# Attention in a four-stage network: two-part fp32r queries and keys, half of the projections among the score units, and DMAs moved between queues

## The reference

```python
attn = softmax(einsum('bhqd,bhkd->bhqk', q * SCALE, k), axis=-1)
out = einsum('bhqk,bhkd->bhqd', attn, v)        # then a projection
```

## Time and profile before

| | |
|---|---|
| median of the runs | 9524.35 us |
| profiled execution | 9521.44 us, span of its core 9519.6 us |
| mean granted TensorE clock | 0.838 of full speed |
| busy: PE, DVE, ACT, POOL | 7285.6, 5233.4, 3309.5, 1466.3 us |
| DMA | 298.52 MB in 158940 packets, mean 31 GB/s |

### The profile page before, as it was taken

One profiled execution on the slowest core, in us unless ns is written; L12 is line 12 of the kernel. 1 busy time (PEld: TensorE's weight loads), 2 busy tenths in 40 slices (PEclk: granted clock), 3 DMA queues, 4 the chain that ended last, 5 costly groups with the idle time before them and its releaser, 6 DMA issues.

```text
span 9519.6 us, 103202 instructions
## 1 busy us (share of the span) xinstructions
PE 7285.6 (77%) x32648; PEld 2877.3 (30%) x32648; DVE 5233.4 (55%) x5444; ACT 3309.5 (35%) x3706; POOL 1466.3 (15%) x700
## 2 busy tenths in 40 slices
PE   6779777797777977679776797777977779777797
PEld 1233322333223332233322333223332233322332
DVE  6575355743566536664366643666536664366643
ACT  3424334243332433324333243332433324333243
POOL 0230002300023010230102301032000320003200
PEclk8879877888887988888888888888988888888888
DMA  2001110011100111001110011100111001110011
GB/s 61 8 27 32 44 43 7 27 32 44 43 7 27 32 44 45 6 27 32 44 45 6 27 32 46 43 5 27 33 46 43 5 27 32 46 43 5 27 33 49
DMA packets 158940, 298.52 MB, mean 31 GB/s; under 512 B 48974, under 2 KB 56390, under 8 KB 158378
## 3 DMA queue, kind: packets, MB, share of 16 engines
q1 hardware_dynamic: 158378, 291.44, 10.2%
HBM read 185.75 MB, written 83.50 MB: 28 GB/s over the span
## 4 chain that ended last, share of the span: by engine, by line
PE 48%; DVE 20%; issue 14%; DMA 5%; DVEq 4%; ACT 4%; SPq 3%; POOL 1%; ACTq 0%; POOLq 0%
PE px L607 10%; PE ring L557 6%; PE ring L584 6%; DVE mx L764 4%; PE ring L560 4%; DVE hs L1262 4%; PE ring L586 3%; PE px L1022 3%; PE ring L1007 3%; DMA ks<-k_split 2%; PE ring L536 2%; PE ring L982 2%; DVE hs L1251 2%; PE ring L996 2%; DVEq L779 2%
## 5 line engine op out<-in xcount | busy, mean ns | idle before, releaser
L764 DVE TENSOR_REDUCE mx<-ring 128x1 f32<-128x1024 f32 (+1 forms) x1920 | 2158.0, 1141 | 2023.8 <-PE ring L560 968.0
L677 ACT ACTIVATE pt<-ring 128x1024 f32<-128x1024 f32 (+1 forms) x1920 | 1874.4, 982 | 2592.8 <-PE ring L586 1109.1
L824 POOL TENSOR_TENSOR os<-oe 64x512 f32<-64x512 f32 x288 | 365.2, 1268 | 6542.8 <-ACT oe L685 6542.8
L607 PE MATMUL px<-pt,vo 128*32 128x512 f32 (+3 forms) x8064 | 1258.4, 616 | 72.8 <-ACT pt L677 72.1
L557 PE MATMUL ring<-kb,qb 96*128 96x512 bf16 x3072 | 1184.3, 430 | 151.0 <-DVE mx L764 80.7
L1307 POOL TENSOR_TENSOR hc<-hs,crep 128x1024 f32<-128x1024 f32 x384 | 1045.4, 2722 | 1460.3 <-DVE hs L1262 1422.0
L584 PE MATMUL ring<-qb,kb 99*128 99x512 bf16 x3072 | 1116.4, 407 | 182.3 <-DVE mx L764 111.9
L560 PE MATMUL ring<-hot,rq 128*128 128x512 f32 x1536 | 901.7, 648 | 0.0
L1262 DVE TENSOR_TENSOR_SCAN hs<-ring,hs 128x1024 f32<-128x1024 f32 x384 | 874.9, 2278 | 1.5 <-ACT ring L1155 1.5
L586 PE MATMUL ring<-rq,hot 128*128 128x512 f32 x1536 | 861.7, 623 | 0.0
L1007 PE MATMUL ring<-duh,spread 96*128 96x512 f32 x1536 | 633.5, 525 | 278.0 <-DVE hs L1251 158.8
(11 more groups left out here) (154 smaller groups left out, 6756.0 us busy)
## 6 DMA issues: line engine op xcount, KB each, us to landing
qs<-q_split SPq DMA_DIRECT2D x192, 128.0 KB
q_parts<-part SPq DMA_DIRECT2D x96, 192.0 KB, 3.5
k_parts<-part SPq DMA_DIRECT2D x96, 192.0 KB, 2.7
qb<-q_parts SPq DMA_DIRECT2D x192, 96.0 KB
kb<-k_parts SPq DMA_DIRECT2D x192, 96.0 KB
ocm<-os SPq DMA_DIRECT2D x576, 32.0 KB
rb<-reciprocals SPq DMA_DIRECT2D x288, 64.0 KB, 2.2
qb<-q_parts SPq DMA_DIRECT2D x192, 64.0 KB
```

The source lines that it names most:

```text
L607: last = nc.tensor.matmul(m.px[32 * g:32 * g + 32, h % 2, lo - f * HF:hi - f * HF], m.vo[:, t, h, :], pt[:, lo - q0:hi - q0], start=t == t ...
L677: nc.scalar.activation(pt, ps, ACT.Exp, scale=1.0 if L == "C" else HD ** -0.5).then_inc(s.pt, 1)
L764: nc.vector.tensor_reduce(out, ps, AX.X, ALU.max).then_inc(s.mx_used, 1)
```

## The change

1. q and k are split in two fp32r parts in A and C as well, as in D. Scores there multiply 48 rows (`qs`, `ks`), weights 50 rows (48 and two of maxima) in place of 96 and 99 bf16 rows. The relative matmuls and D's masks are as before. Maxima have two parts everywhere. The ones under the keys come by DMA at the start of A and C.
2. Only jobs 0 and 1 are done before the first score. `LATE` puts the token projections (two units of four tiles) and jobs 2 and 3 with A's rotations in ring slots among the score units 2 to 11. All four head loads are issued together, before jobs 2 and 3 are split.
3. In C and D ACT writes `hi` straight from PSUM and DVE `lo` from PSUM; in A ACT writes `hi` from the rotated tile. The copies of v to `vo` move from DVE to ACT. The v bias is folded into the projection's bias at the start of the program.
4. The cosine product of the rotation moves from DVE to POOL.
5. In A and C `values` stands before each odd-numbered weights unit (from 3 on), not after each even-numbered one.
6. Of `px` ACT copies one half (`odd`), and DVE adds the other from PSUM to `os`. POOL issues the result's DMAs to `ocm`, SP the denominators' alone, on a semaphore of their own.
7. In C the position rows for D are loaded into each buffer after its last head, at h = 8 to 11, not at h = 2 to 5.

```diff
-STORED = {"A": (16 * 6, 16 * 6), "C": (16 * 10, 16 * 6), "D": (16 * 4, 16 * 4)}
+STORED = 16 * 4
...
+LATE = {2: ("tokens", 0), 4: ("tokens", 1), 6: ("job", 2), 8: ("rotated", 2), 9: ("job", 3), 11: ("rotated", 3)}
...
-                last = nc.tensor.matmul(out[:, half], m.qb[u][0:BR, q], m.kb[u][0:BR, half],
+                last = nc.tensor.matmul(out[:, half], m.qs[u][0:QR, q], m.ks[u][0:QR, half],
                                         start=True, stop=L == "A")
...
-                last = nc.tensor.matmul(out[:, half], m.kb[u][:, k], m.qb[u][:, half], start=True, stop=L == "A")
+                last = nc.tensor.matmul(out[:, half], m.ks[u][0:QR + MR, k], m.qs[u][0:QR + MR, half],
+                                        start=True, stop=L == "A")
...
+    for i in range(2):
+        job(i)
+    if L == "A":
+        for i in range(2):
+            rotated(i)
...
     for n in range(total + lead):
+        for kind, i in late(L, n):
+            if kind == "tokens":
+                tokens(i)
+            if kind == "job":
+                job(i)
+            if kind == "rotated":
+                rotated(i)
         for h, axis in relatives(L, n):
             relative(h, axis)
...
+            if L != "D" and g % 2 == 1 and g >= 3:
+                values(*divmod(g // 2 - 1, steps // 2))
             weights(g)
             if L == "D" and g >= 1:
                 values(*divmod(g - 1, steps))
-            if L != "D" and g % 2 == 0 and g >= 2:
-                values(*divmod(g // 2 - 1, steps // 2))
...
-        nc.scalar.activation(m.oe[h % 2][:, 0, :], m.px[0:64, h % 2, :], ACT.Copy)
-        nc.scalar.activation(m.oe[h % 2][:, 1, :], m.px[64:P, h % 2, :], ACT.Copy).then_inc(s.oe, 1)
+        nc.scalar.activation(m.odd[h % 2][:], m.px[64:P, h % 2, :], ACT.Copy).then_inc(s.odd, 1)
...
+    def outputs(h):
+
+        dve.wait_ge(s.odd, NH * b + h + 1)
+        if h >= 2:
+            dve.wait_ge(s.o_in, OUT_IN * (NH * b + h - 1))
+            dve.wait_ge(s.dn_in, OUT_IN * (NH * b + h - 1))
+        nc.vector.tensor_tensor(m.os[h % 2][:], m.px[0:64, h % 2, :], m.odd[h % 2][:], ALU.add).then_inc(s.os, 1)
...
+    def cosine(i):
+
+        pool.wait_ge(s.raw, 4 * b + i + 1)
+        if i >= 2:
+            pool.wait_ge(s.rotated, 4 * b + i - 1)
+        nc.gpsimd.tensor_tensor(m.ra[i % 2][:], m.raw[i % 2][:], m.cos[:], ALU.mult).then_inc(s.cosine, 1)
...
+        for f in range(NHF):
+            nc.gpsimd.dma_start(m.ocm[HD * i:HD * (i + 1), c, f * HF:(f + 1) * HF],
+                                m.os[h % 2][32 * f:32 * f + HD, :]).then_inc(s.o_in, 16)
```

More of the change, by code:

```diff
@@ L405, with late @@
 JOBS = [(0, 0), (1, 0), (0, 1), (1, 1)]
+VTILES = 4
+LATE = {2: ("tokens", 0), 4: ("tokens", 1), 6: ("job", 2), 8: ("rotated", 2), 9: ("job", 3), 11: ("rotated", 3)}
+def late(L, n):
+    unit = LATE.get(n)
+    return [unit] if unit and (L == "A" or unit[0] != "rotated") else []
 def spans(L):
@@ L433, in ring @@
 def ring(L):
-    units = []
+    units = [("job", 0), ("job", 1)] + ([("rotated", 0), ("rotated", 1)] if L == "A" else [])
     for n in range(UNITS[L] + LEAD[L]):
+        units += late(L, n)
         for h, axis in relatives(L, n):
@@ new lines, in low @@
+    def low(i):
+        which, c = JOBS[i]
+        dve.wait_ge(s.hi, 4 * b + i + 1)
+        if i >= 2:
+            dve.wait_ge(s.stored[i % 2], STORED * b + STORED // 2)
+        hi, lo = m.hi[i % 2][:].bitcast(F32), m.lo[i % 2][:]
+        if L == "A":
+            nc.vector.tensor_tensor(lo, m.raw[i % 2][:], hi, ALU.subtract).then_inc(s.lo, 1)
+        elif L == "C":
+            nc.vector.scalar_tensor_tensor(lo, m.ring[0:CP, slot[("job", i)], :],
+                                           w.qkb[:, 2 * which + c:2 * which + c + 1], hi,
+                                           ALU.add, ALU.subtract).then_inc(s.lo, 1)
+        else:
+            nc.vector.tensor_tensor(lo, m.ring[0:CP, slot[("job", i)], :], hi, ALU.subtract).then_inc(s.lo, 1)
@@ L796, in attn_vector @@
             scores(n)
+        for kind, i in late(L, n - 1):
+            if kind == "rotated":
+                low(i)
+        for kind, i in late(L, n):
+            if kind == "rotated":
+                rotated(i)
+            if kind == "job" and L != "A":
+                low(i)
         for h, axis in relatives(L, n):
@@ L907, in spread @@
             sp.dma_start(m.rb[HD * i:HD * (i + 1), c, :], src).then_inc(s.rb_in, 16)
+    if L != "D":
+        sp.wait_ge(m.norm.stats, len(LAYERS) * b + LAYERS.index(L) + 1)
+        for u in range(NBUF):
+            sp.dma_start(m.ks[u][QR:QR + MR, :].bitcast(F32), m.one).then_inc(s.ones_in, 16)
     for i in range(2):
-        split(i, *JOBS[i])
+        split(i)
     for i in range(2):
-        sp.wait_ge(s.stored[i], STORED[L][i] * b + FIRST_STORED[L][i])
-    load(0)
+        sp.wait_ge(s.stored[i], STORED * b + STORED // 2)
+    for u in range(NBUF):
+        load(u)
+    maxima(0)
     for i in range(2, 4):
-        split(i, *JOBS[i])
-    load(1)
-    for h in (2, 3):
-        sp.wait_ge(s.heads[h % 2], HEAD_IN[L] * (NH // 2 * b + 1))
-        load(h)
-    for i in range(2):
-        sp.wait_ge(s.stored[i], STORED[L][i] * (b + 1))
-    maxima(0)
+        split(i)
     for h in range(NH):
@@ L931, in attn_sync @@
             spread(0)
-        if L == "C" and 2 <= h < 2 + NBUF:
-            sp.dma_start(m.qs[h - 2][QR:DR, :].bitcast(F32), m.far).then_inc(m.rows_in, 16)
-            sp.dma_start(m.ks[h - 2][QR:DR + MR, :].bitcast(F32), m.near).then_inc(m.rows_in, 16)
+        if h == HC - NBUF:
+            for i in range(2):
+                sp.wait_ge(s.stored[i], STORED * (b + 1))
         if h + NBUF < NH:
```

412 lines of the change are left out of this document (211 added, 201 removed).

## The result

The changed kernel takes 13098.1 us (median of two runs) where the kernel before takes 9524.4: the ratio is 1.375, with a 95% interval of 1.3725 to 1.3775. It is 37% slower, and the forecast was 9155 us, 4% faster. Its profiled execution has a span of 13100.1 us.

The account below looks back on a forecast made before the run. No engine was full: a chain through three ring slots paced A, PE itself bounded C. Gains of 15 in A, 22.1 in C, 8.6 in D, 45.7 us an image, 366 for eight, took 9524.4 to about 9155 us (range 8930 to 9430).

Parts of the forecast that it names:

- rival (c): Slower: 48 active rows hold the clock down in A and C; 10030 us, chance 0.08.
- Part 2: In A and C, two-part fp32r streams like three-part bf16; each burst that starts cold costs 0.12 us.
- the dips: In C, the clock falls to 0.51 once a head, costing 3.4 us; 3 of 11 forecast to vanish, 10 us.
- slow pair in A: A pair of units at the lower clock lasts about 2.05 us longer; half of A's 48 pairs would cost 49 us.
- A long stretch: In A (attention with rotation), a head falls from 15.2 to 14.5 us, 8.4 us less an image.
- The cold burst: In A, an fp32r burst after values or a wait can't hide its first load: 0.12 us, twice a pair.
- C long stretch: In C (attention with relative positions), filled waits save 10.1 us and fewer clock dips 10 us an image.
- The 0.92 us of waits: In C, moved values fill waits of 1.0 and 0.4 us, less 0.48 for exposed loads: net 0.92 us a head.
- rival (a): The clock dips in C go altogether, 27 us more an image: 8940 us, chance 0.15.
- Heads and leads: Stage starts up to the first weights unit: with two jobs before the first score, A gains 4 us, C 1.
- D: 7x7 neighbourhood attention: head and lead 0, long stretch 6 by earlier load issue, end 2.6: 8.6 us less an image.
- Ends of A and C: Fewer copies, adds and DMA issues before the last reciprocal: 2.6 us less in A, 1 in C after table loads.

Follow-up runs that it names:

- 96 and 98 rows: The changed kernel with scores and weights in A and C padded with zeros to 96 and 98 rows; 9343.5 us, ratio 0.9807.
- 66 rows: The changed kernel with scores and weights in A and C padded with zeros to 66 and 68 rows; 9769.9 us.
- the kernel with 112 rows: The changed kernel with fp32r scores and weights in A and C padded with zeros to 112 and 114 rows; 9291.0 us, ratio 0.9754.
- Part 1 alone: The kernel before with only the values block moved ahead of a pair's second weights unit in A and C; 9220.7 us, ratio 0.9681.
- a second part: The kernel before with values moved ahead in A and C, and POOL issuing each head's two output stores; 9104.3 us, ratio 0.955.
- 64/66: The changed kernel with scores and weights in A and C padded with zeros to 64 and 66 rows; 11433.6 us.

## Why the prediction was wrong

The forecast was 9155 us (8930 to 9430) with a chance of 0.75 for faster by over 2%. The case that came, rival (c), had 0.08 and a price of 10,030 us.

**The step that failed is Part 2, "Both stream alike".** It compared formats and left the rows out: what 48 rows in place of 96 do to the clock, and to whether a load is hidden, stood in the sum as nothing. Measured, the two are 474 us an image: the clock at 0.50 in A and C, and 0.29 us for each load in C. The number that could have warned stood in the text: B's 96-row matmuls at 0.50 with PE busy without a gap. It warned that a busy PE is not enough for the higher clock. It does not show that rows were B's reason, since A's matmuls with 96 and 98 rows ran at 0.98. Nor is it so that the trace of before had no matmul of 48 rows: the relative ones of C have 48, 32 columns wide, and the dips to 0.51 stood behind them. Whether their rows had a part in the dips is not shown. I read B's row as evidence for (c), and then gave (c) 0.08, because C's alternation with 128 rows does rise. That half was sound (C at 66 rows has 0.92, A 0.63 to 0.81), but it holds only where the loads stay hidden.

**Rival (c) had one of the two mechanisms, and not its size.** Its price of a slow pair in A was right: 3.56 + 2.05 = 5.61 us, which with the transpose is 22.7 us a head, and 22.6 were measured. It let half of A's pairs run so, and all did. In C it put the clock at 0.75, and it was 0.50. And it had no term for loads in the open: 208 us an image, the largest single piece. Part 2 let only the first load of a burst stand in the open, 0.12 us for four bursts a head in C; with 48 or 50 rows beside 128, all 64 were exposed. The Trainium skill has the rule that comes nearest on another page than the one that I weighed (the tiling page, above). The page that I did weigh (TensorE: Matmul & The Clock Gate, LDWEIGHTS) says that a load's time does not depend on its rows, and the trace agrees: 0.28 and 0.29 us for 50 and 128 rows. Its figure, columns/1.2 ns or 0.107 us for 128, fits the bf16 loads (0.10) and not the fp32r ones, which took 0.28 to 0.29 us at the lower clock and 0.18 to 0.19 at the higher; the measurement decides. The page answers how long a load lasts, not whether anything hides it.

The other steps can be judged on the kernel with 112 rows, where the rows are out of the way. It took 9291 us, 136 above the forecast. By stages it won 6.5 us an image in A (forecast 15), 8.3 in C (22.1) and 13.6 in D (8.6), and 3.1 in B, where nothing was forecast (medians of eight images).

- **A long stretch: nearly right.** 14.5 us a head forecast, 14.57 measured as the median over heads and images; the stretch as a whole lost 6.4 us where 8.4 were forecast. By the runs apart: order 1.3 us in bf16, fp32r 0.6 back. The cold burst was put at 0.12 us; if all of the 0.63 us is theirs, it is 0.63 / 8 = 0.08.
- **C long stretch: right for the wrong reason.** 20 us less forecast, 14 measured (290.0 to 275.8). The 0.92 us of waits did not come, since the wait moved to the next unit; the dips, of which I gave a part, all but went, as rival (a) said. Both prices were too high. Forecast and rival (a) together gave the dips 11 x 3.4 = 37 us, on top of the waits; with Part 1 alone, in bf16, the whole stretch won 22.7 (290.0 to 267.2). There were seven to nine dips and not eleven, and some lasted 3.4 us and not 6.8. The fp32r loads take 0.7 us a head of it back (23.2 to 23.9 on average).
- **Heads and leads: forecast too short by 6 us in A and 8 in C.** From x ready to the first weights matmul, A took 69.7 us (64.1 forecast, 68.3 before) and C 76.9 (68.5 forecast, 70.0 before). Half of it or more is the time to the first score, 33.7 us in A for 29.6 and 31.2 in C for 27. It was added up with a load that lands 3.7 us after its issue, 5.9 us from the first issue to use. That was a misreading: the 3.7 us in the earlier trace rows are of the stores into `q_split`, and the trace gives no landing time for the loads. What they took stood in the trace of before all the same. D's first load is issued at 2248.04, and its first score starts here:

```profile
2256.71 0.64 PE L553 MATMUL ring<-ks,qs 112*128 112x320 f32 x1 [2.52 <-DMA ks<-k_split]
```

  That is 8.7 us, for one head's load. In the changed kernel four heads' loads are issued one behind the other, 16 DMAs, and it takes ten, in C as in D:

```profile
2385.74 1.09 SPq L940 DMA_DIRECT2D qs<-q_split  x2
2386.87 1.07 SPq L940 DMA_DIRECT2D ks<-k_split  x2
...
2395.73 1.86 PE L549 MATMUL ring<-qs,relh 48*32 48x32 f32 x32 [15.81 <-DMA ks<-k_split]
```

  So 2.8 us of the miss are the misread row, and about 1.3 may be the other heads' loads, which no run shows by itself. The rest is the leads: 36.0 us in A for 34.5, and 45.7 in C for 41.5. C's lead grew by 17.6 us, so the 4.1 us of idle PE that should have taken in some of the late work did not.
- **D: better than forecast.** 13.6 us for 8.6: head and lead 3.4 (0 forecast), long stretch 4.6 (6 forecast, and PE's waits for loads fell from 15.3 to 8.4 us in the third image), tail 4.3 (2.6).
- **Ends of A and C: right**, 2.5 and 1.3 us for 2.6 and 1.
- **The forecast's own test worked.** A mean clock below 0.85 in the long stretches of A or C was named as what would make it wrong.

## What to carry to other kernels

Before cutting the contraction rows of a matmul to save work or bytes, ask what stands beside it: at 64 rows and below, alternating with more than 64, its load is no longer hidden, and few rows can hold TensorE at 1.2 GHz even when it hardly idles. Rows of zeros add no columns to stream (matmuls of 512 columns stood 0.23 to 0.24 us apart with 66 rows and with 112) and bought 3807 us here. This was seen in one kernel, with matmuls of 128 x 512; what carries over is the question, and a run with padded rows answers it. And price each part of a change alone: one line of this one was worth 3.2%, and with a second part 4.5%, inside a change that cost 37%.

## What the runs showed of the hardware that was not expected

- The same 741 instructions of A's long stretch ran at a mean granted clock of 0.50 with 48/50 and 64/66 rows, 0.64 with 66/68 (third image; 0.63 to 0.81 over the eight), 0.98 with 96/98 and 112/114, while PE was busy for 98, 99, 96, 90 and 90% of it. A low clock makes PE busy for longer, so the high share is no cause; it shows that being busy was not enough. What in the array the clock follows is open.
- Between 64 and 66 rows beside 128-row matmuls, a pair's spacing changes from 0.43 to 0.24 us at the higher clock.
- Moving the small waits in C's sequence, with their sum unchanged (21.7 and 21.2 us), removed all dips of its clock but one: 17.7 us of PE's busy time in one stretch.
